# Edge layers of a graph network: the radial weights of two tiles as two products of 64 rows, one on each half of the array, in place of one product with a block-diagonal matrix

## The chip, the cores and the metric

The kernel runs on one core of a Trainium2 chip. Its time is the device time of one execution in microseconds, lower is better. Before the change three runs gave 8992.46 (the median), 9030.67 and 8966.20 us. Engines are named as the profile names them: PE is TensorE's matmul, PEld its weight load, DVE VectorE, ACT ScalarE, POOL GpSimd, SP SyncE.

## The reference, cut to what matters

Four message-passing layers over 50,000 nodes and 50,000 edges in float32. Layers 1 to 3 have a stage over the edges. Their part that the change touches is the small network that turns each edge's scalars into the weights of its message:

```
h = silu(edge_scalars @ (Wfc1 / sqrt(fan)))      # fan 16, 8 or 64 -> 64
w = h @ (Wfc2 / sqrt(64))                        # 64 -> 192 (layers 1, 2) or 224 (layer 3)
mid0 = w0 * e0 * sh0                             # parts of w times the gathered node row
...
sums = segment_sum(mid, edge_dst)                # then small matrices
```

Everything else (layer norms, node stages, the attention of layer 0) is the same before and after.

## The kernel before, in words

Edges come in 98 chunks of 512, a chunk being four tiles of 128 edges. Each stage of the program is one pass over the 98 chunks, with a software pipeline written out by hand: every engine has a list of steps with a delay in chunks, and the steps of one round are issued in the order of that list. The loop is unrolled four chunks deep. The edge stages of layers 1, 2 and 3 are `edge_layer` (L408 on), each followed by a short `join` and a node stage. The order of an edge round of chunk t is:

- SP: `load_edges(t)` (edge indices L426, then, once `message(t-2)` is done, the destination rows L324, attributes L433 and edge scalars L435), then `store_sums(t-4)` (L332), which waits for ACT's copy of the result.
- POOL: `gather(t)`, four indirect DMAs (L451), after the indices of t are in.
- PE: `hidden(t)` (L466, one product with a block-diagonal first matrix, after the edge scalars are in), `sums(t-2)` (L486, 12 products of 128 columns, 16 in layer 3), `weights(t)` (L474), `second(t-3)` (L498, L500, L503 in layer 3, L505).
- ACT: the silu (L516), the copies of the sums (L534), in layer 3 a copy in the gathered rows (L522), `weights(t)`: the copy of the radial weights out of PSUM (L526), and the copy of the result (L539).
- DVE: `message(t-1)` (L357 to L380, on to L388 in layer 3), then `prepare(t)`: the segment matrix (L337) after `sums(t-2)`, and the attributes (L555), which wait for the gathered rows of t.

The scalars of a chunk lie in pairs of tiles: rows 0 to 63 of `hid_p` (after the silu) hold the hidden values of tiles 0 and 2, rows 64 to 127 those of tiles 1 and 3, each in 128 columns for one tile; columns 0 to 127 are tiles 0 and 1, columns 128 to 255 tiles 2 and 3. `fc2_` is a matrix of 128 rows with Wfc2 twice on its diagonal (`diagonal(fc2, fc2)`), so one product of 128 rows and 2*w_cols columns (384, in layer 3 448) gives both tiles of a pair. `hid_p` is the stationary operand, `fc2_` the moving one. Each float32 product stands in the trace as two passes, each a weight load and a matmul; 1176 passes for 588 products.

Of the kernel before, what the change touches and what calls it, by code (L numbers as in the profile page):

```python
# [26 lines left out]
P = 128  # L27
# [96 lines left out]
def pipeline(eng, chunks, stages):  # L124


    most = max(d for _, d in stages)
    lead = most + (-most) % 4
    rounds = (chunks - lead) // 4

    def static(t):
        for stage, d in stages:
            if 0 <= t - d < chunks:
                stage(Step(t - d, t - d, (t - d) // 2, (t - d) // 4))

    for t in range(lead):
        static(t)
    with eng.Fori(0, rounds) as i:
        for k in range(4):
            for stage, d in stages:  # L140
                c = lead + k - d
                stage(Step(i * 4 + c, c, i * 2 + c // 2, i + c // 4))
    for t in range(lead + 4 * rounds, chunks + most):
        static(t)
# [7 lines left out]
def gnn_kernel(nc, inp, out):  # L152
# [5 lines left out]
    def sb(name, shape, dt=F32, own=None):  # L158

        return (own or ctx).enter_context(nc.sbuf_tensor(name, shape, dt))  # L160

    def two(name, shape, dt=F32, own=None):
        return [sb(f"{name}_{k}", shape, dt, own) for k in range(2)]
# [16 lines left out]
    with ctx:  # L180
# [13 lines left out]
        def W(name, rows=None, cols=None):  # L194
            r, c = SHAPES[name]
            r0, r1 = rows or (0, r)
            c0, c1 = cols or (0, c)
            return w_all[r0:r1, OFFSETS[name] + c0:OFFSETS[name] + c1]
# [12 lines left out]
        radial = two("radial", [P, TILES, 224])  # L211
# [7 lines left out]
        psum = ctx.enter_context(nc.psum_tensor("banks", [P, 8, 512], F32))  # L219

        def bank(k, rows=P, cols=512):
            return psum[0:rows, k, 0:cols]
# [12 lines left out]
        def tiled(k, cols):  # L235

            return psum[:, k:k + 2, :].rearrange("p b (t c) -> p (b t) c", t=2)[:, :, 0:cols]
# [77 lines left out]
        def precompute(eng, *values):  # L315


            for v in values:
                if type(v) is not int:
                    eng.compute_val(v)  # L320
# [87 lines left out]
        def edge_layer(layer):  # L408
            fan, radial_scale, w_cols, parts, v_at = LAYERS[layer]
# [4 lines left out]
            with ExitStack() as own, nc.Block() as block:  # L414
                erow = [sb(f"erow_{layer}_{k}", [P, TILES, EROW + 65], own=own) for k in range(4)]
                mid = two(f"mid_{layer}", [P, TILES, parts * P], own=own)
                mid_t, hid_p = two(f"mid_t_{layer}", [P, parts, CHUNK], own=own), sb(f"hid_p_{layer}", [P, 2 * P], own=own)
# [40 lines left out]
                @block.tensor  # L458
                def _(pe):
                    def hidden(s):  # L460

                        precompute(pe, edge_in[s.slot].after(s.half + 1), hid_sb.after(s.g))
                        pe.wait_ge(ready.sem, 1)
                        pe.wait_ge(edge_in[s.slot].sem, edge_in[s.slot].after(s.half + 1))
                        pe.wait_ge(hid_sb.sem, hid_sb.after(s.g))
                        pe.matmul(bank(1, P, 2 * P), W(f"fc1_{layer}"), scal_e[s.slot][:, :],  # L466
                                  start=True, stop=True).then_inc(hid_mm.sem, 1)

                    def weights(s):

                        pe.wait_ge(hid_sb.sem, hid_sb.after(s.g + 1))
                        pe.wait_ge(w_sb.sem, w_sb.after(s.g))
                        for k in range(2):
                            last = pe.matmul(psum[:, 2 + k, 0:2 * w_cols], hid_p[:, k * P:(k + 1) * P],  # L474
                                             W(f"fc2_{layer}"), start=True, stop=True)
                        last.then_inc(w_mm.sem, 1)

                    def sums(s):

                        pe.wait_ge(mid_step.sem, mid_step.after((s.g + 1) * steps))  # L480
                        pe.wait_ge(agg_sb.sem, agg_sb.after(parts * s.g))
                        for k in range(parts):
                            if k == 3:
                                pe.wait_ge(agg_sb.sem, agg_sb.after(parts * s.g + 1))
                            for t in range(TILES):
                                last = pe.matmul(psum[:, SEG[k], t * P:(t + 1) * P],  # L486
                                                 mid[s.slot][:, t, k * P:(k + 1) * P], seg[s.slot][:, t, :],
                                                 start=True, stop=True)
                            last.then_inc(agg_mm.sem, 1)

                    def second(s):

                        pe.wait_ge(agg_sb.sem, agg_sb.after(parts * (s.g + 1)))
                        pe.wait_ge(res_sb.sem, res_sb.after(s.g))
                        post = tiled(6, AGG)
                        for t in range(TILES):
                            cut = slice(t * P, (t + 1) * P)
                            pe.matmul(post[:, t, 0:v_at + 96], mid_t[s.slot][:, 0, cut], W(f"pa{layer}"),  # L498
                                      start=True, stop=False)
                            pe.matmul(post[:, t, v_at:v_at + 96], mid_t[s.slot][:, 1, cut], W(f"pb{layer}"),  # L500
                                      start=False, stop=False)
                            if crossed:
                                pe.matmul(post[:, t, v_at:v_at + 96], mid_t[s.slot][:, 3, cut], W("pd3"),  # L503
                                          start=False, stop=False)
                            last = pe.matmul(post[:, t, v_at + 32:v_at + 96], mid_t[s.slot][:, 2, cut], W(f"pc{layer}"),  # L505
                                             start=False, stop=True)
                        last.then_inc(post_mm.sem, 1)

                    pipeline(pe, chunks, [(hidden, 0), (sums, 2), (weights, 0), (second, 3)])

                @block.scalar
                def _(act):
                    def hidden(s):
                        act.wait_ge(hid_mm.sem, hid_mm.after(s.g + 1))
                        act.wait_ge(w_mm.sem, w_mm.after(s.g))
                        act.activation(hid_p[:, :], bank(1, P, 2 * P), ACT.Silu, scale=radial_scale) \  # L516
                            .then_inc(hid_sb.sem, 1)

                    def weights(s):
                        if crossed:  # L520
                            act.wait_ge(rows_in[s.slot].sem, rows_in[s.slot].after(s.half + 1))
                            act.activation(erow[s.quad][:, :, EROW:EROW + 64], erow[s.quad][:, :, 1 + C0:1 + C0 + 64],  # L522
                                           ACT.Copy).then_inc(wrap_sb.sem, 1)
                        act.wait_ge(w_mm.sem, w_mm.after(s.g + 1))
                        act.wait_ge(mid_step.sem, mid_step.after((s.g - 1) * steps))
                        act.activation(radial[s.slot][:, :, 0:w_cols].rearrange("p (b t) c -> p b t c", b=2),  # L526
                                       psum[:, 2:4, 0:2 * w_cols].rearrange("p b (t c) -> p b t c", t=2), ACT.Copy) \
                            .then_inc(w_sb.sem, 1)

                    def sums(s):  # L530
                        act.wait_ge(post_mm.sem, post_mm.after(s.g - 1))
                        for k in range(parts):
                            act.wait_ge(agg_mm.sem, agg_mm.after(parts * s.g + k + 1))
                            act.activation(mid_t[s.slot][:, k, :], bank(SEG[k]), ACT.Copy).then_inc(agg_sb.sem, 1)  # L534

                    def second(s):
                        act.wait_ge(post_mm.sem, post_mm.after(s.g + 1))
                        act.wait_ge(sums_out[s.slot].sem, sums_out[s.slot].after(s.half))
                        act.activation(res[s.slot][:], tiled(6, v_at + 96), ACT.Copy) \  # L539
                            .then_inc(res_sb.sem, 1)  # L540

                    pipeline(act, chunks, [(hidden, 0), (sums, 2), (weights, 0), (second, 3)])

                @block.vector
# [1708 lines left out]
```

## Time and profile before

| | |
|---|---|
| time, median of three runs | 8992.46 us (8966.20 to 9030.67) |
| span of the profiled execution, first to last instruction | 8623.9 us |
| PE busy | 6524.1 us, 76% |
| PEld busy | 5791.9 us, 67% |
| DVE busy | 6173.8 us, 72% |
| POOL busy | 5083.8 us, 59% |
| ACT busy | 4113.7 us, 48% |
| edge stages of layers 1, 2, 3, about | 3960 to 4770, 5390 to 6190, 6985 to 7950 us of the span |

No time of its own stands with the profiled execution beyond its span; 368.6 us of the median lie outside that span. A busy share is an average over stages with different limits. Matmuls overlap and their ends are modelled, so how long a pass holds the engine is read from the distance of its start to the next one's, not from its duration.

### The profile page before, as it was taken

Reading aid. Unit: us, or ns where it says so; the run is one execution under the profiler, and the core shown is the slowest. Engines: PE = TensorE matmul, PEld = TensorE weight load, DVE = VectorE, ACT = ScalarE, POOL = GpSimd, SP = SyncE. Lnnn points to the kernel's source line nnn. Section 1 sums busy time; section 2 is a strip of 40 time slices with the busy share of each in tenths; the row PEclk is TensorE's granted clock in tenths of the full one; section 3 lists DMA queues with packets and bytes.
Section 4 is the critical chain, followed back from the end, with each engine's and each line's share of the span. In section 5 each row is a group of like instructions: output and inputs, shape, how many; then the busy total and the mean of one; then the engine's idle time right before and its main releaser. Section 6 shows DMA issues by size and latency. Waiting matters only on the chain. (4 is left out here: it accounts for less than half of the span.)

```text
span 8623.9 us, 182979 instructions
## 1 busy us (share of the span) xinstructions
PE 6524.1 (76%) x42580; PEld 5791.9 (67%) x42580; DVE 6173.8 (72%) x20276; ACT 4113.7 (48%) x9706; POOL 5083.8 (59%) x4620
## 2 busy tenths in 40 slices
PE   3667878775456888888999666999755579998555
PEld 2555666664446888887888566888755569998454
DVE  4666888886556888885665777566588867775777
ACT  1334555552223444454444677444466654544444
POOL 4667888884334555554554787555466644443777
PEclk9887888885558999999999888999888889999666
DMA  6883333336883333333554676444455544443555
GB/s 129 173 179 81 88 88 88 88 90 128 161 164 96 104 101 105 101 105 102 126 125 118 190 211 203 118 122 124 115 169 165 168 125 120 120 119 105 157 160 154
DMA packets 910283, 1117.55 MB, mean 130 GB/s; under 512 B 458518, under 2 KB 546422, under 8 KB 910032
## 3 DMA queue, kind: packets, MB, share of 16 engines
q1 hardware_dynamic: 728032, 812.69, 34.1%
q0 software_dynamic: 182144, 303.64, 15.7%
q8 instruction: 42, 0.69, 0.0%
q14 instruction: 65, 0.53, 0.0%
HBM read 650.35 MB, written 465.65 MB: 129 GB/s over the span
## 5 line engine op out<-in xcount | busy, mean ns | idle before, releaser
L451 POOL DMA_INDIRECT erow<-e_rows,edge_idx x1176 | 1245.5, 1059 | 1232.0 <-issue 1136.5
L671 POOL DMA_INDIRECT agg<-seg_rows,edge_idx x1568 | 1550.7, 989 | 664.2 <-issue 473.0
L720 POOL TENSOR_TENSOR stats<-stats,power 128x8 f32<-128x8 f32 (+1 forms) x588 | 757.6, 1289 | 730.9 <-DVE stats L708 306.2
L400 PE MATMUL banks<-w_all,xt 128*128 128x128 f32 (+1 forms) x2352 | 538.3, 364 | 642.8 <-DVE y_more L945 146.1
L486 PEld LDWEIGHTS banks<-seg,mid 128*128 128x128 f32 x7840 | 931.9, 194 | 15.6
L486 PE MATMUL banks<-seg,mid 128*128 128x128 f32 x7840 | 932.9, 277 | 0.0
L400 PEld LDWEIGHTS banks<-w_all,xt 128*128 128x128 f32 x2352 | 422.3, 243 | 725.6 <-issue 713.0
L534 ACT ACTIVATE mid_t<-banks 128x512 f32<-128x512 f32 x980 | 585.2, 597 | 316.5 <-PE banks L486 314.2
L403 PE MATMUL banks<-w_all,xt 128*128 128x128 f32 x3528 | 642.0, 332 | 0.0
L403 PEld LDWEIGHTS banks<-w_all,xt 128*128 128x128 f32 x3528 | 603.8, 248 | 0.0
L498 PE MATMUL banks<-w_all,mid_t 128*128 128x161 f32 (+1 forms) x2352 | 583.5, 330 | 2.8 <-ACT res L539 2.8
L539 ACT ACTIVATE res<-banks 128x644 f32<-128x644 f32 (+1 forms) x294 | 218.1, 742 | 687.4 <-PE banks L505 672.5
L1207 POOL DMA_INDIRECT work<-src_table,edge_idx x392 | 460.3, 1174 | 108.1 <-issue 108.1
L608 POOL DMA_INDIRECT row_of_dram<-where_back x196 | 245.5, 1252 | 386.4 <-DMA where_back<-place_dram 339.6
L738 ACT ACTIVATE xo<-y,stats 128x64 f32<-128x64 f32 (+1 forms) x1200 | 428.9, 442 | 72.3 <-DVE stats L727 67.4
L1207 POOL DMA_INDIRECT y<-dst_table,edge_idx x392 | 386.6, 986 | 119.4 <-issue 119.1
L474 PE MATMUL banks<-w_all,hid_p 128*128 128x384 f32 (+1 forms) x1176 | 454.2, 508 | 3.1 <-ACT hid_p L516 3.1
L738 ACT ACTIVATE xo<-y_more,stats 128x64 f32<-128x64 f32 (+1 forms) x1152 | 411.5, 442 | 72.7 <-DVE stats L727 72.1
L498 PEld LDWEIGHTS banks<-w_all,mid_t 128*128 128x128 f32 x2352 | 378.7, 191 | 89.2 <-issue 38.4
L505 PE MATMUL banks<-w_all,mid_t 128*128 128x64 f32 x2352 | 423.4, 262 | 0.0
L500 PE MATMUL banks<-w_all,mid_t 128*128 128x96 f32 x2352 | 420.8, 260 | 0.0
L337 DVE TENSOR_TENSOR seg<-dst_row,edge_idx 128x512 f32<-128x512 int32 x294 | 202.8, 690 | 272.2 <-PE banks L486 233.5
(275 smaller groups left out, 18230.6 us busy)
## 6 DMA issues: line engine op xcount, KB each, us to landing
x_rows<-xo SPq DMA_DIRECT2D x294, 324.0 KB
xin<-x_rows SPq DMA_DIRECT2D x294, 324.0 KB
e_rows<-ets SPq DMA_DIRECT2D x294, 322.0 KB
dst_row<-in_dst_flat SPq DMA_DIRECT2D x294, 256.0 KB
xin<-in_x SPq DMA_DIRECT2D x196, 324.0 KB
seg_rows<-res SPq DMA_DIRECT2D x196, 322.0 KB, 2.6
seg_rows<-res SPq DMA_DIRECT2D x98, 384.0 KB, 2.4
seg_rows<-res SPq DMA_DIRECT2D x98, 338.0 KB, 9.4
```

What stands on the lines that cost most here:

```text
L400: pe.matmul(flat[:, to + k * cols:to + (k + 1) * cols], of[:, k * P:(k + 1) * P], W(w_s), start=True, stop=True)
L403: last = pe.matmul(flat[:, to + 2 * cols + k * P:to + 2 * cols + (k + 1) * P], of[:, (2 + k) * P:(3 + k) * P], W(w_v), start=True, stop=True)
L451: pool.indirect_dma_start(erow[s.quad][:, t, 0:EROW], None, table, bass.IndirectOffsetOnAxis(idx[s.slot][:, t:t + 1], 0),).then_inc(rows_i ...
L474: last = pe.matmul(psum[:, 2 + k, 0:2 * w_cols], hid_p[:, k * P:(k + 1) * P], W(f"fc2_{layer}"), start=True, stop=True)
L486: last = pe.matmul(psum[:, SEG[k], t * P:(t + 1) * P], mid[s.slot][:, t, k * P:(k + 1) * P], seg[s.slot][:, t, :], start=True, stop=True)
L498: pe.matmul(post[:, t, 0:v_at + 96], mid_t[s.slot][:, 0, cut], W(f"pa{layer}"), start=True, stop=False)
L505: last = pe.matmul(post[:, t, v_at + 32:v_at + 96], mid_t[s.slot][:, 2, cut], W(f"pc{layer}"), start=False, stop=True)
L534: act.activation(mid_t[s.slot][:, k, :], bank(SEG[k]), ACT.Copy).then_inc(agg_sb.sem, 1)
L671: pool.indirect_dma_start(agg[s.quad][:, t, 0:SUM_COLS[layer]], None, seg_rows[layer], bass.IndirectOffsetOnAxis(idx[s.slot][:, t:t + 1], ...
L720: pool.tensor_tensor(st[:, at + n:at + 2 * n], st[:, at:at + n], power[:, 0:n], ALU.pow) \
L738: last = act.activation(to, of if at == 0 else of.rearrange("p (i c) -> p i c", i=3), ACT.Identity, bias=st[:, 40 + t:41 + t], scale=st[:, ...
L1207: pool.indirect_dma_start(to[s.slot][:, t, :], None, table, bass.IndirectOffsetOnAxis(idx[s.slot][:, first + t:first + t + 1], 0),).then_i ...
```

## The change

In `weights` of PE, the two products of 128 rows and 2*w_cols columns become four of 64 rows and w_cols columns. The half h of the rows (0 to 63 or 64 to 127) is multiplied with the block of `fc2_` on the same rows; half h writes into bank 2 + h, at columns k*w_cols of it. Before, the pair k wrote into bank 2 + k. So the order of tiles within the two banks is another one, and ACT's copy (one instruction, as before) writes its halves into other tiles of `radial`. Semaphores and the order of steps are the same.

```
 for k in range(2):
-    last = pe.matmul(psum[:, 2 + k, 0:2 * w_cols], hid_p[:, k * P:(k + 1) * P],
-                     W(f"fc2_{layer}"), start=True, stop=True)
+    for h in range(2):
+        last = pe.matmul(psum[:, 2 + h, k * w_cols:(k + 1) * w_cols],
+                         hid_p[h * 64:(h + 1) * 64, k * P:(k + 1) * P],
+                         W(f"fc2_{layer}", (h * 64, h * 64 + 64), (h * w_cols, h * w_cols + w_cols)),
+                         start=True, stop=True)
 last.then_inc(w_mm.sem, 1)
...
-act.activation(radial[s.slot][:, :, 0:w_cols].rearrange("p (b t) c -> p b t c", b=2),
+act.activation(radial[s.slot][:, :, 0:w_cols].rearrange("p (t b) c -> p b t c", b=2),
                psum[:, 2:4, 0:2 * w_cols].rearrange("p b (t c) -> p b t c", t=2), ACT.Copy)
```

## Rows read from the trace of the kernel before

**Rows 1.** Stretches of the three edge stages: length, busy time (count), clock, DMA share, GB/s.
```profile
core 0: us, PE busy (x) PEld busy (x) DVE busy (x) ACT busy (x) POOL busy (x), PEclk, DMA share, GB/s
4000.00:4600.00 600.00, 574.42 (x4191) 524.54 (x4190) 372.49 (x930) 281.76 (x465) 322.33 (x310) 1.00 0.51 126
5500.00:6100.00 600.00, 573.56 (x4170) 523.33 (x4170) 372.34 (x930) 281.37 (x464) 327.61 (x311) 0.99 0.50 123
7100.00:7800.00 700.00, 700.00 (x5170) 641.78 (x5170) 510.64 (x1183) 346.38 (x591) 317.46 (x295) 1.00 0.42 119
```

**Rows 2.** Timeline of PE in layer 1 (start, us, engine, line; merged), one round.
```profile
4301.31 2.84 PE L486 MATMUL banks<-seg,mid 128*128 128x128 f32 x24
4303.98 1.46 PE L474 MATMUL banks<-w_all,hid_p 128*128 128x384 f32 x4
4305.28 0.44 PE L498 MATMUL banks<-w_all,mid_t 128*128 128x161 f32 x2
4305.56 0.36 PE L500 MATMUL banks<-w_all,mid_t 128*128 128x96 f32 x2
4305.75 0.36 PE L505 MATMUL banks<-w_all,mid_t 128*128 128x64 f32 x2
4305.94 0.49 PE L498 MATMUL banks<-w_all,mid_t 128*128 128x161 f32 x2
```

**Rows 3.** The same in layer 3; the last row is the next round.
```profile
7302.05 0.65 PE L466 MATMUL banks<-scal_e,w_all 128*128 128x256 f32 x2
...
7306.11 1.67 PE L474 MATMUL banks<-w_all,hid_p 128*128 128x448 f32 x4
...
7307.62 0.49 PE L498 MATMUL banks<-w_all,mid_t 128*128 128x192 f32 x2
...
7311.54 0.65 PE L466 MATMUL banks<-scal_e,w_all 128*128 128x256 f32 x2
```

**Rows 4.** Waits in layer 3, 7100 to 7800 us (total us, times, longest).
```profile
DVE tmp L357 <- ACT radial L526: 132.6, 74, 1.9
...
DVE seg L337 <- PE banks L486: 50.7, 74, 0.7
```

**Rows 5.** Waits in layer 1, 4000 to 4600 us.
```profile
DVE attr L555 <- DMA erow<-e_rows,edge_idx: 123.7, 61, 5.0
...
PE banks L466 <- issue: 25.4, 33, 2.5
```

**Rows 6.** Timeline of layer 1 that ends in a late round.
```profile
4316.91 0.65 PE L466 MATMUL banks<-scal_e,w_all 128*128 128x256 f32 x2
...
4324.20 0.65 PE L466 MATMUL banks<-scal_e,w_all 128*128 128x256 f32 x2
...
4325.34 0.36 SPq L332 DMA_DIRECT2D seg_rows<-res  x1
...
4326.31 0.34 SPq L426 DMA_DIRECT2D edge_idx<-in_edge_idx  x1
...
4331.39 1.17 POOL L451 DMA_INDIRECT erow<-e_rows,edge_idx  x1 [4.26 <-issue]
...
4335.37 1.36 POOL L451 DMA_INDIRECT erow<-e_rows,edge_idx  x1 [0.30 <-issue]
...
4339.44 0.18 DVE L555 TENSOR_TENSOR attr<-attr,erow 128x24 f32<-128x24 f32 x1 [3.52 <-DMA erow<-e_rows,edge_idx]
...
4343.51 0.28 DVE L380 TENSOR_TENSOR mid<-radial,tmp 128x128 f32<-128x128 f32 x1
...
4344.02 0.33 SPq L324 DMA_DIRECT2D dst_row<-in_dst_flat  x1
...
4345.11 0.36 SPq L435 DMA_DIRECT2D scal_e<-in_scal_e  x1
...
4347.96 0.67 PE L466 MATMUL banks<-scal_e,w_all 128*128 128x256 f32 x2 [0.80 <-issue]
```

**Rows 7.** Timeline of the setup: products of 2 rows alternate with products of 128 rows.
```profile
87.67 1.22 PE L1975 MATMUL banks<-w_all 2*128 2x256 f32 x2
...
88.82 0.50 PEld L1976 LDWEIGHTS banks<-w_all 128*128 128x128 f32 x2 [0.65 <-issue]
88.82 1.22 PE L1976 MATMUL banks<-w_all 128*128 128x256 f32 x2
89.97 0.50 PEld L1975 LDWEIGHTS banks<-w_all 2*128 2x128 f32 x2 [0.65 <-issue]
89.97 1.22 PE L1975 MATMUL banks<-w_all 2*128 2x256 f32 x2
```

**Rows 8.** Durations, ns min/median/max, of two lines with 256 columns.
```profile
L1976 PE MATMUL banks<-w_all x8: 634/714/796, 86.5 to 94.0; 128*128 128x256 f32 x8
...
L466 PE MATMUL banks<-scal_e,w_all x588: 378/435/767, 3960.6 to 7909.6; 128*128 128x256 f32 x196
```

**Rows 9.** The setup as a stretch, columns as in rows 1.
```profile
80.00:95.00 15.00, 9.46 (x18) 4.67 (x18) 6.34 (x28) 0.00 (x0) 0.00 (x0) 1.00 0.00 1
```

## The prediction

> **What bounds the kernel now.** I read the stretches of the three edge stages first, since only they run the changed line [rows 1]. The reader is to see that PE is busy for the whole 700 us of layer 3, at clock 1.00, while DVE has 511 and POOL 317; in layers 1 and 2 it is busy for 574 of 600. Next the timeline, for the length of a round. In layer 3 one round is 7302.05 to 7311.54, 9.49 us, and PE has no gap in it [rows 3]; DVE waits twice in each round, for the radial weights (132.6 us in 74 rounds, 1.8 each) and for PE's sums (0.7) [rows 4]. So layer 3 is PE's alone, and what PE's round gains or loses the stage gains or loses.
>
> Layers 1 and 2 are of another kind. 310 gathers in 600 us are 77.5 rounds of four, so a round is 7.74 us; a round without a wait is 7.29 (4316.91 to 4324.20) [rows 6]. PE waits before `hidden` in 33 of some 78 rounds, 25.4 us together, and DVE waits 123.7 us in 61 rounds for gathered rows [rows 5]. One late round shows the chain [rows 6]: PE starts a round at 4324.20, and with that the result of the round before can be copied; the store is issued at 4325.34, the indices at 4326.31, the gathers run from 4331.39 to 4336.73, their rows release DVE at 4339.44, the message ends at 4343.79, this lets SP issue the loads from 4344.02 to 4345.11, and `hidden` starts at 4347.96. That is 23.76 us for three rounds, 7.92 each, and no product of `weights` lies in it. I walked back so from the last round of either stage: one round where PE hadn't waited, three where the message had waited for gathered rows. There are 48 such chains as this one, and of 184 rounds about 40 are PE's. A saving of PE is worth a quarter of itself here (49 of 196 rounds), and less as the saving grows; a loss is worth more and more of itself, about half at 0.3 us.
>
> **The change part by part.**
>
> Streams. The four passes of `weights` take 4303.98 to 4305.28, 1.30 us, in layers 1 and 2, so 0.325 a pass of 384 columns [rows 2]; in layer 3 7306.11 to 7307.62, 1.51 us, 0.378 a pass [rows 3]. After, there are eight passes of half the columns, 0.163 and 0.189. If nothing overlaps their sum is as before, 1.30 and 1.51. The columns alone would allow half, 0.65 and 0.75, if the two halves always ran side by side.
>
> Loads. Each pass brings its weight load, so there are four loads more in a round. 24 passes of 128 columns take 4301.31 to 4303.98, 0.111 each, and passes of 96 and of 64 columns follow one another equally fast (4305.56, 4305.75, 4305.94: 0.095 each): below some 100 columns the load is what is left [rows 2]. I take 0.11 for a load of 128 columns. Then eight passes can't start closer than 0.11: seven such steps and the last stream are 0.77 + 0.16 = 0.93 us, in layer 3 0.77 + 0.19 = 0.96, beside 1.30 and 1.51. In the order of the program both passes of a half follow each other and can't overlap, only the second of one half with the first of the other; laid out so, it is 0.94 and 0.99. I take these if the halves overlap at all. Bounds: nothing overlaps (1.30, 1.51), or loads overlap too (0.65, 0.75).
>
> Going over to 64 rows and back. The hot rounds have no such product, the setup has: two passes of 2 rows, two of 128, in turns [rows 7]. They start 1.15 us apart (87.67, 88.82, 89.97), and each time the load starts together with its matmul, after a gap of 0.65, where in the rounds loads run ahead of matmuls. Two passes of 256 columns at 0.325 for 384 are 0.43 at the full clock. The granted clock in the setup reads 1.00 [rows 9], but its passes last 714 ns where those of 256 columns in the edge stages last 435 at the full clock and at most 767 [rows 8], so I read the setup as running at the half clock: 0.87 for the two passes, 0.28 for going over. At the full clock I halve it, 0.14, as the passes themselves about halve (767 to 435); 0.28 is the upper bound, and zero the lower one, if 64 rows need no going over. The round has two of them: 0.28 us, bounds 0 and 0.56.
>
> The Trainium skill says on this, in TensorEngine Tiling (Array Packing), Key Properties, that a change of tiling mode drains TensorE; the trace agrees by the gap of 0.65 us in front of each load. By that rule without a price the sum keeps its term and not its size.
>
> ACT's copy reads the same banks with the same shape and writes the same number of values, and SP, POOL and DVE issue what they did. They cost nothing new. The copy starts when the last product ends, earlier or later with it, and DVE's next wait, 1.8 us for the radial weights in layer 3, moves along. DVE is busy for 6.9 of 9.49 us in a round (510.64 in 73.8 rounds) and stays free of the bound for any change below 1 us.
>
> Sum, with overlap and 0.28: layers 1 and 2, 0.94 + 0.28 = 1.22 for 1.30, -0.08; layer 3, 0.99 + 0.28 = 1.27 for 1.51, -0.24. In layer 3 this counts for about 96 of 98 rounds: -23 us. In layers 1 and 2 it counts for 49 of 196: -4 us. Together -27 us, on a span of 8623.9 that would be 8597; with the 368.6 us outside it the median of 8992.5 becomes 8965.
>
> **The rivals.**
>
> A. *No side-by-side work (slower).* The two halves run one after the other, because both passes of a float32 product hold it or because the halves share the stream. Then 0.28 a round is lost outright, from the first round on: layer 3 96 x 0.28 = 27 us, layers 1 and 2 half of 196 x 0.28 = 27 us, 54 together, 9047. It decides as soon as the overlap gives less than 0.28 us a round. For it: all passes on one engine stream in order, and no row of this trace shows two side by side. Against it: the two halves use different rows and different banks. With the upper price, 0.56, PE's round in layers 1 and 2 becomes 7.86 and passes the 7.74 of today; three quarters of 196 x 0.56 are 82, layer 3 54: +136, 9128. With overlap but the upper price it is +0.20 and +0.04: 20 + 4, 9016.
>
> B. *Overlap and no going over.* -0.36 and -0.52 a round: layers 1 and 2 45 x 0.36 = 16, layer 3 96 x 0.52 = 50, together -66, 8926. Against it speaks the gap in the setup, though that is for 2 rows, not 64.
>
> C. *Pairs run as one.* Both halves' loads and streams side by side, 0.65 and 0.75, no going over: -0.65 x 40 and -0.76 x 96 give -26 and -73, -99, 8893. With going over paid it is -0.37 and -0.48: -17 and -46, 8929. In layer 3 the loads by SP and the gather chain would have to hold a round of 8.7 us; their chain in layers 1 and 2 takes 7.92 a round, and with the longer message (DVE has 6.9 us a round for 4.8 [rows 1], so 2.1 more in three rounds) some 8.6, so I leave the gain whole.
>
> The Trainium skill has this one as a rule: in TensorE: Matmul & The Clock Gate, Part 3, products on different row groups run concurrently and start about 4 ns apart. No row of this trace shows it. The same part says that a load overlaps a running matmul only on other row groups; here the trace differs, as 24 passes on all 128 rows follow one another at 0.111 us with their loads under the stream before.
>
> D. *Nothing lands.* Layers 1 and 2 hide everything and layer 3's terms cancel: 8992.
>
> **How the numbers follow.** My forecast, overlap limited by loads with going over paid: 0.38. Overlap with the upper price or terms that cancel (D): 0.16. A at the lower price 0.18, at the upper 0.06. B and C with going over paid, 0.15. C in full 0.07. The predicted time is 8965. Its own range is 8940 to 8990. The range for 8 in 10 takes in 8893 at one end, without the case's own scatter, and A at the lower price at the other, with some 15 us of scatter: 8890 to 9062. About 1%, 90 us, is what a measurement of this kernel can tell from no change (its three runs span 64 us). Faster by more than that is C and a part of the scatter of B: 0.11. Slower by more is A at the upper price and part of the lower one: 0.10. Within: 0.79.
>
> **What the profile after would show.** From the first pass of L474 to L498 in layer 3: 1.27 us if I am right, 1.79 in rival A, 0.99 in B, 0.75 in C. The round of layer 3 is then 9.25, or 9.77, 8.97, 8.73, the same in each of its rounds. A gap in front of the first load of 64 rows and of the first of 128 rows shows the going over. In layers 1 and 2 rounds without a wait start 7.2 apart, PE waits before `hidden` longer than 25.4 us in 600, and the mean round stays above 7.6. Wrong would be a round of layer 3 that isn't PE's any more, a granted clock in the edge stages below 0.97, or a `weights` longer than 1.8 us.

## The result: half a per cent faster, and where it is in the profile after

Over 20 runs each the changed kernel takes 8941.58 us (8898.14 to 8998.47) and the kernel before 8987.16 (8920.23 to 9077.81); the ratio is 0.9948, 95% interval 0.9929 to 0.9968, or 45 us less (29 to 64). In a later measurement, 12 runs against 29, it was 8886.46 to 8926.31, ratio 0.9964 (0.9940 to 0.9989); the ratio leaves out two slow runs of the 29.

The spans of the two profiles don't show this: 8623.9 us before, 8936.7 after. The profiled execution after took 8938.53 us, so only 1.8 us lie outside its span. My 368.6 us outside the span of before was a misreading: that execution was itself a short one, by some 360 us, and no other run of the kernel before, of these 20 and those 29, took less than 8833.08. Most of it lies in code before layer 1 that the change doesn't touch: layer 1 starts at 3961 us of the span before and at 4294 after (last section). The comparison therefore goes stage by stage.

First the stretches of the three edge stages after the change (length, busy time and count of PE, PEld, DVE, ACT and POOL, clock, DMA share, GB/s), as [rows 1] are for before.

```profile
4400.00:5000.00 600.00, 562.57 (x4541) 524.77 (x4538) 378.02 (x940) 268.47 (x471) 325.49 (x313) 1.00 0.51 127
5800.00:6400.00 600.00, 560.51 (x4515) 522.30 (x4513) 378.84 (x940) 265.79 (x468) 324.40 (x311) 1.00 0.50 124
7400.00:8100.00 700.00, 695.76 (x5589) 658.94 (x5588) 520.59 (x1206) 341.08 (x606) 324.90 (x301) 1.00 0.46 123
```

In layer 3 PE, busy for all of 700 us before, now has gaps. Then the timeline of PE in one round of layer 3, the answer to [rows 3].

```profile
7722.48 0.65 PE L466 MATMUL banks<-scal_e,w_all 128*128 128x256 f32 x2
7722.96 3.73 PE L489 MATMUL banks<-seg,mid 128*128 128x128 f32 x32
7726.63 1.03 PE L475 MATMUL banks<-w_all,hid_p 64*128 64x224 f32 x8
7727.59 0.59 PE L501 MATMUL banks<-w_all,mid_t 128*128 128x192 f32 x2
...
7731.61 0.65 PE L466 MATMUL banks<-scal_e,w_all 128*128 128x256 f32 x2
```

The round is 9.13 us for 9.49. Its three parts: from `hidden` to `weights` 4.15 for 4.06 (+0.09), from `weights` to `second` 0.96 for 1.51 (-0.55), from there to the next `hidden` 4.02 for 3.92 (+0.10). Eight passes of 224 columns at 0.189 would be 1.51 us in a row, and they take at most 0.96 with the way back to 128 rows in it: the halves run side by side. The starts of the single passes, which the merged line hides, show it directly: they come in pairs 0.007 us apart (7726.627 and 7726.634), and the pairs follow one another at 0.189 (7726.921, 7727.110, 7727.299). Layer 1 shows the same, as in [rows 2]:

```profile
4654.13 0.92 PE L475 MATMUL banks<-w_all,hid_p 64*128 64x192 f32 x8
4654.98 0.54 PE L501 MATMUL banks<-w_all,mid_t 128*128 128x161 f32 x2
4655.35 0.36 PE L503 MATMUL banks<-w_all,mid_t 128*128 128x96 f32 x2
```

0.85 for 1.30, and 0.37 for 0.28 to L503 after it. Rounds without a wait take 7.05 us for 7.29.

What becomes of it is in the waits: first layer 1, 4400 to 5000 us (total us, times, longest), the answer to [rows 5].

```profile
DVE attr L558 <- DMA erow<-e_rows,edge_idx: 61.5, 51, 3.9
...
PE banks L466 <- issue: 32.9, 41, 1.6
```

PE waits longer before `hidden`, 32.9 us for 25.4, and DVE half as long for gathered rows, 61.5 for 123.7. Neither can be put down to the change: the second profile of the kernel before (below) has 17.8 and 56.0 in 4500 to 5100 us. Then layer 3, 7400 to 8100 us, the answer to [rows 4]:

```profile
DVE tmp L357 <- ACT radial L529: 86.7, 70, 1.3
DVE seg L337 <- PE banks L489: 73.1, 73, 3.5
...
ACT res L542 <- remote: 26.8, 6, 4.9
```

The last line is not in the same view of the first profile, but the change didn't bring it. The second profile of the kernel before has it more often, in 7600 to 8200 us:

```profile
ACT res L539 <- remote: 135.4, 29, 5.1
```

ACT's copy of the result waits for PE's last product of `second` and for the store of two chunks before. I read "remote" as that store landing late, and planned the three experiments with four buffers by it. The semaphore updates in the traces say otherwise. In all 6 of these waits after, and in all 29 of before_again, the update that the copy starts on, 0.02 to 0.11 us ahead of it, is PE's, and the store's semaphore had its last one over 15 us earlier. (The trace doesn't keep every update, but the copy starts as far behind PE's as in rounds without such a wait: in after, signal at 7581.01 and copy at 7581.11.) PE's last product of `second` had by its record ended 1.55 to 2.16 us before that signal. So the late thing is PE's signal and not a transfer. In the first profile PE's signals come at most 0.02 us after the product, in layer 1 (4000 to 4600 us) as in layer 3 (7100 to 7800).

Each stage from the first to the last start of `hidden`, 97 rounds, read from the timelines, with the best round of each (the first four rounds, in which the pipeline fills, left out; rows of the table that belong to the experiments are used below):

| kernel | layer 1 | layer 2 | layer 3 | best rounds, layers 1 and 3 |
|---|---|---|---|---|
| before | 751.8 | 749.4 | 920.0 | 7.29, 9.49 |
| after | 744.4 | 744.2 | 900.0 | 7.05, 9.14 |
| before_again | 752.7 | 749.9 | 951.9 | 7.29, 9.49 |
| full_split | 762.8 | 775.5 | 962.0 | 7.31, 9.50 |
| one_half | 777.1 | 765.2 | 963.6 | 7.69, 9.89 |
| half_by_half | 760.2 | 768.1 | 922.1 | 7.05, 9.14 |
| after_again | 754.8 | 741.6 | 900.3 | 7.04, 9.14 |
| narrow | 752.6 | 743.5 | 907.4 | 7.04, 9.13 |
| after_store5 | 769.0 | 750.5 | 937.0 | 7.04, 9.14 |
| before_store5 | 742.3 | 717.6 | 922.5 | 7.29, 9.49 |
| only3 | 761.8 | 756.7 | 915.0 | 7.29, 9.14 |
| after_res4 | 767.8 | 754.4 | 915.5 | 7.05, 9.14 |
| after_deep | 802.6 | 774.5 | 944.1 | 7.04, 9.14 |
| before_deep | 725.1 | 775.1 | 927.5 | 7.29, 9.49 |

The best rounds of one kernel agree to 0.02 us between executions. The lengths of the stages differ by up to 3.5% between two executions of one kernel (layer 3 of before and before_again). Between the first two profiles the three stages are 7.4, 5.2 and 20.0 us shorter, 33 together, which lies in the interval of the runs.

### The profile page after: what moved, and what is told of

Its sections match the earlier page's. It is cut to its first block and busy times, and to the rows that moved or that the text cites. A ratio compares the mean times of both kernels' runs of the same rounds, so it can differ in the third digit from the quotient of the medians.

```text
span 8936.7 us, 185331 instructions
## 1 busy us (share of the span) xinstructions
PE 6648.0 (74%) x43756; PEld 5967.4 (67%) x43756; DVE 6182.5 (69%) x20276; ACT 4070.6 (46%) x9706; POOL 5067.3 (57%) x4620
## 5 line engine op out<-in xcount | busy, mean ns | idle before, releaser
L489 PEld LDWEIGHTS banks<-seg,mid 128*128 128x128 f32 x7840 | 937.0, 194 | 35.3 <-issue 14.7
L537 ACT ACTIVATE mid_t<-banks 128x512 f32<-128x512 f32 x980 | 543.4, 599 | 442.1 <-PE banks L489 403.5
L501 PE MATMUL banks<-w_all,mid_t 128*128 128x161 f32 (+1 forms) x2352 | 613.5, 343 | 2.8 <-ACT res L542 2.8
L1210 POOL DMA_INDIRECT y<-dst_table,edge_idx x392 | 443.2, 1131 | 119.5 <-issue 119.1
L1210 POOL DMA_INDIRECT work<-src_table,edge_idx x392 | 404.2, 1031 | 109.1 <-issue 109.1
L503 PE MATMUL banks<-w_all,mid_t 128*128 128x96 f32 x2352 | 421.1, 260 | 0.0
L1217 POOL TENSOR_TENSOR stats<-stats,power 128x12 f32<-128x12 f32 (+2 forms) x100 | 226.5, 2265 | 327.0 <-DVE stats L1404 302.3
L1291 PE MATMUL banks<-w_all,mid 128*128 128x128 f32 (+1 forms) x1176 | 180.7, 294 | 304.5 <-ACT mid_t L1357 241.5
```

The lines of the kernel that those rows point to most:

```text
L489: last = pe.matmul(psum[:, SEG[k], t * P:(t + 1) * P], mid[s.slot][:, t, k * P:(k + 1) * P], seg[s.slot][:, t, :], start=True, stop=True)
L1210: pool.indirect_dma_start(to[s.slot][:, t, :], None, table, bass.IndirectOffsetOnAxis(idx[s.slot][:, first + t:first + t + 1], 0),).then_i ...
```

## The experiments

Two theories on the step that decides. Mine at first: halves overlap, but loads and the order of the passes keep `weights` at 0.94 and 0.99 us. The rival: both halves run with loads and all side by side, 0.65 and 0.75, and going over costs more. The merged lines of the profile after can't tell which part of its 1.05 us (0.96, and 0.09 ahead of it) is stream and which is going over. So: the kernel before once more; more loads without 64 rows; 64 rows without anything to run beside; the order changed; the halves made unequal.

**before_again.** No edit.

> The kernel before, once more, to see what of the two profiles differs without any change. If the edge stages are as fixed as they look, the round of layer 3 is again 9.49 us in over 90 of its rounds, the mean rounds of layers 1 and 2 are 7.6 to 7.9, and the stage of layer 0 over the edges (650 to 2000 us in the first profile, 650 to 2300 in the one of the changed kernel) takes one of these two lengths. If the difference of the two layer-0 stages were caused by the change, this run would show the short one.

9083.16 us, beside 9161.21 for another run of the same kernel on that chip. Layers 1 and 2 are as in the first profile, and the stage of layer 0 took the long form without the change. But layer 3 was at its best round in 40 of 97 rounds, where the first profile had 94: I expected over 90. Layer 3 belonging to PE alone was true of one execution, not of the kernel. How a late round comes about can be read there: PE's signal of `second` comes 2.16 us after its product (7605.62), ACT's copy starts at 7607.89 after 5.14 us, the silu and ACT's copies of the sums come behind it, and PE stands for 0.73 us ahead of a product of `sums` (7609.51).

**full_split.** Eight passes on 128 rows.

```
-last = pe.matmul(psum[:, 2 + k, 0:2 * w_cols], hid_p[:, k * P:(k + 1) * P], W(f"fc2_{layer}"), ...)
+for h in range(2):
+    last = pe.matmul(psum[:, 2 + k, h * w_cols:(h + 1) * w_cols], hid_p[:, k * P:(k + 1) * P],
+                     W(f"fc2_{layer}", None, (h * w_cols, h * w_cols + w_cols)), ...)
```

> The kernel before with each product of weights split by its columns only: four products of 128 rows and w_cols columns, so eight passes and eight loads, no 64-row mode. Theory: loads hide under streams of 192 columns, so the round of layer 3 stays 9.49 us (weights 1.50), of layers 1 and 2 at best 7.29. Rival, if a load costs even beside a stream: 4 more loads at 0.11 give 9.93 and 7.73.

9209.49 us in one run. PE's timeline in layer 3:

```profile
8001.94 1.68 PE L475 MATMUL banks<-w_all,hid_p 128*128 128x224 f32 x8
8003.46 0.49 PE L500 MATMUL banks<-w_all,mid_t 128*128 128x192 f32 x2
```

1.52 us for eight passes, best rounds 7.31 and 9.50: four loads more cost 0.01 to 0.02 us. Loads on all 128 rows lie under the streams before them.

**one_half.** All four products on rows 0 to 63.

```
-hid_p[h * 64:(h + 1) * 64, k * P:(k + 1) * P], W(f"fc2_{layer}", (h * 64, h * 64 + 64), (h * w_cols, ...))
+hid_p[0:64, k * P:(k + 1) * P], W(f"fc2_{layer}", (0, 64), (0, w_cols))
```

> The changed kernel with all four products on rows 0 to 63 (the half of rows 64 to 127 is computed from the wrong half, so those values are not the reference's). Same passes, same going over to 64 rows and back, nothing that could run side by side. Theory (halves run side by side, worth half the stream; going over twice costs 0.40): layer 3 loses 0.75 against the changed kernel, round 9.89 us, weights from the last sum to the first product of second 1.90; layers 1 and 2 at best 7.70. Rival (the 64-row form is itself faster, or the going over cheaper, and nothing runs side by side): round 9.14 as in the changed kernel.

9184.85 us in one run. Layer 3:

```profile
8001.82 0.65 PE L466 MATMUL banks<-scal_e,w_all 128*128 128x256 f32 x2
8002.31 3.73 PE L489 MATMUL banks<-seg,mid 128*128 128x128 f32 x32
8005.97 1.78 PE L475 MATMUL banks<-w_all,hid_p 64*128 64x224 f32 x8
8007.68 0.59 PE L501 MATMUL banks<-w_all,mid_t 128*128 128x192 f32 x2
...
8011.71 0.65 PE L466 MATMUL banks<-scal_e,w_all 128*128 128x256 f32 x2
```

The round is 9.89, as the theory had it, and 1.71 between L475 and L501 for 0.96. The 0.75 between them is exactly half of the stream: the halves overlap fully. And 9.89 - 9.49 = 0.40 (in layer 1, 7.69 - 7.29 = 0.40) is the price of going over and back, with the same streams in both kernels. The starts of the single passes split it evenly. Going over, the first pass starts 0.205 us after the last of `sums` for the usual 0.112, and the second 0.294 after the first for 0.189; going back, the steps are 0.279 for 0.189 and 0.267 for 0.162. That is 0.20 us each way, and half of it is the second pass waiting: the load of the first starts together with its pass (8005.971 and 8005.973), it doesn't run ahead.

**half_by_half.** The loops swapped.

```
-for k in range(2):
-    for h in range(2):
+for h in range(2):
+    for k in range(2):
```

> The changed kernel with the two loops swapped: both products of rows 0 to 63 first, then both of rows 64 to 127, result the same. In program order only one pair of passes of different halves is adjacent. Theory A (the engine starts matmuls in program order, pairs need neighbours): of eight passes only one pair overlaps, weights takes 7 x 0.188 + 0.40 = 1.72, round of layer 3 9.7 us. Theory B (a half runs ahead of the other independently): 0.75 + 0.40, round 9.14 as in the changed kernel.

9126.94 us in one run, and theory B: 0.96 us again, best rounds 7.05 and 9.14.

```profile
8009.05 1.03 PE L475 MATMUL banks<-w_all,hid_p 64*128 64x224 f32 x8
8010.01 0.59 PE L501 MATMUL banks<-w_all,mid_t 128*128 128x192 f32 x2
```

Two whole products of one half precede the first of the other in the program, and still the first two passes start 0.013 us apart (8009.048 and 8009.061). My premise that only neighbouring passes can pair is wrong.

**narrow.** Only 64 columns in the products of rows 64 to 127.

```
+n = 64 if h else w_cols
-last = pe.matmul(psum[:, 2 + h, k * w_cols:(k + 1) * w_cols], ..., W(f"fc2_{layer}", ..., (h * w_cols, h * w_cols + w_cols)), ...)
+last = pe.matmul(psum[:, 2 + h, k * w_cols:k * w_cols + n], ..., W(f"fc2_{layer}", ..., (h * w_cols, h * w_cols + n)), ...)
```

> The changed kernel with only 64 of the w_cols columns in the products of rows 64 to 127 (the rest of those radial weights is not computed). Theory (the halves are two arrays with a queue each, the longer one sets the time): best rounds stay 7.05 and 9.14. Rival 1 (halves alternate in time and share the stream): 256 of 384 columns are left, weights is shorter by a third of 0.65, rounds 6.83 and 8.9. The durations of the 64-column passes also show which pass goes beside which.

8879.26 us in one run. Layer 3:

```profile
8009.89 1.02 PE L476 MATMUL banks<-w_all,hid_p 64*128 64x224 f32 x8
8010.84 0.59 PE L502 MATMUL banks<-w_all,mid_t 128*128 128x192 f32 x2
```

0.95 us, best rounds 7.04 and 9.13. The longer half sets the time; the halves don't share a stream.

Then the second question, where PE's saving goes: 0.24 x 196 + 0.35 x 98 = 81 us on PE, 45 in the runs. My theory was the gather chain, begun by indices that queue on SP behind a store that waits for PE.

**after_again.** No edit, measured beside the next two.

> The changed kernel beside the three others of this call, for their comparison. Theory: its best rounds are 7.05, 7.05 and 9.14 us again; how far the mean of a stage lies above its best round is set by the gathered rows, not by PE. It should be 30 to 60 us faster than the kernel before.

8886.46 us, 40 less than before (8926.31), or 32 by the ratio 0.9964. The best rounds are as expected. That gathered rows set the distance of the mean from them is not shown: layer 3 has 8 of the waits for PE's late signal in 500 us.

**after_store5** and **before_store5.** One edit, on the changed kernel and on the kernel before.

```
-pipeline(sp, chunks, [(load_edges, 0), (lambda s: store_sums(sp, s, s.g, layer, res), 4)])
+pipeline(sp, chunks, [(load_edges, 0), (lambda s: store_sums(sp, s, s.g, layer, res), 5)])
```

> The changed kernel with SP's store_sums one round later (delay 5 for 4), so that the load of the next indices doesn't queue behind a store that waits for PE's second. Theory (the gather chain hides PE's saving): the indices go out some 4 us earlier, the chain is off, and the mean rounds fall to within 0.2 us of the best ones, 7.1 to 7.25 and 9.15 to 9.3: about 0.5 x 196 + 0.1 to 0.5 x 98, 100 to 150 us faster than the changed kernel. Rival (the late rounds come from the DMA rings or from GpSimd's own pace, not from SP's order): mean rounds stay at 7.6 and above, no change.

> The kernel before with the same edit of SP's order. Theory: mean rounds 7.35 to 7.5 and 9.5 to 9.6, 70 to 110 us faster than before; and between this kernel and the changed one with the same edit the change is worth nearly its whole saving on PE, 0.24 x 196 + 0.35 x 98 = 81 us, where without the edit it is worth 30 to 60. Rival: the change's worth with the edit is the same 30 to 60.

On the kernel before: 8864.03 us, ratio 0.9950 (0.9919 to 0.9980), layers 1 and 2 at 742.3 and 717.6 us with mean rounds of 7.65 and 7.40. They are within 0.05 us of the best round in 67 and 87 rounds, in the two profiles without the edit in 39 to 43, so the chain was part of what held them. On the changed kernel: 8930.83, ratio to before 1.0028 (0.9998 to 1.0058), 44 us slower than without the edit. There too more rounds are at the best one (45 and 55 for 32 and 33), but nine rounds behind the fill take 11 to 15 us, where before_store5 has one. The wait in one of the nine, in layer 1:

```profile
4557.96 0.24 SPq L435 DMA_DIRECT2D scal_e<-in_scal_e  x1
...
4558.83 0.71 ACT L542 ACTIVATE res<-banks 128x644 f32<-128x644 f32 x1 [6.50 <-remote]
4559.44 0.38 ACT L519 ACTIVATE hid_p<-banks 128x256 f32<-128x256 f32 x1
4559.94 1.65 PE L475 MATMUL banks<-w_all,hid_p 64*128 64x192 f32 x8 [2.28 <-issue]
```

ACT stands for 6.50 us before the copy of a result, and the silu and PE's `weights` stand behind it. The store that the copy could wait for had its last update 11.3 us earlier; what comes at 4558.73 is PE's signal of `second`, whose last product had ended at 4553.90. In the 600 us from 4300 on PE's signals are up to 4.8 us late here and up to 4.6 in before_store5, so why the changed kernel has the long rounds and the other not is open. Both expectations failed: the edit gains 62 us on the kernel before, short of 70, and nothing on the changed one. So did the one that it brings out the change's full worth: with the edit the change costs 67 us (8864.03 to 8930.83), where without it it gains 40.

**after_res4**, **after_deep** and **before_deep.** Four result buffers for two, with four semaphores for the stores; in the two deep ones the store one round later as well.

```
-res = two(f"res_{layer}", [P, TILES, SUM_COLS[layer]], own=own)
+res = [sb(f"res_{layer}_{k}", [P, TILES, SUM_COLS[layer]], own=own) for k in range(4)]
...
-act.wait_ge(sums_out[s.slot].sem, sums_out[s.slot].after(s.half))
-act.activation(res[s.slot][:], tiled(6, v_at + 96), ACT.Copy) \
+act.wait_ge(sums_quad[s.quad].sem, sums_quad[s.quad].after(s.quarter))
+act.activation(res[s.quad][:], tiled(6, v_at + 96), ACT.Copy) \
```

> The changed kernel with four result buffers but the store in its old place. Theory (the indices still queue behind a store that waits for PE): layers 1 and 2 stay at mean rounds of 7.5 to 7.7; layer 3, where ACT waited for stores (8 waits, 34 us in 500), loses its late rounds and comes to 890 us. Rival (the buffers alone are enough): 7.1 to 7.25 in layers 1 and 2 too.

> The changed kernel with SP's store one round later and, besides, four result buffers for two, so that ACT's copy of a result waits for the store of four chunks ago and not of two. Theory (with the later store alone ACT waited for late stores, and with the old order the gather chain bound): both are off, the mean rounds come to within 0.2 us of the best, 7.05 to 7.25 and 9.15 to 9.3, the three stages 690 to 710 and 890 to 905 us, in all 100 us or more below the kernel before. Rival (late rounds come from DMA landing times, wherever they are waited for): stages stay near 745, 745, 900.

> The same two edits on the kernel before. Theory: rounds 7.29 to 7.4 and 9.49 to 9.6, stages 715, 712 and 925 us; the changed kernel with the same edits is then 60 to 81 us faster than this one, against 32 to 46 us without them. Rival: the distance stays at 32 to 46, so PE's saving is lost in something else than SP's order and the two result buffers.

9293.16, 9331.60 and 9220.75 us beside 9156.93 of the kernel before: ratios 1.0133 (1.0101 to 1.0165), 1.0153 (1.0107 to 1.0199) and 1.0071 (1.0042 to 1.0101). A good part of that lies in code ahead of layer 1 that none of them edits: `hidden` of layer 1 starts at 4530, 4519 and 4517 us, in only3, measured beside them, at 4403. Why, I can't say; the four further semaphores are the one thing I know of that reaches there, and no run has them alone. But the edge stages gained nothing either: after_res4 has 767.8, 754.4 and 915.5 us where only3 has 761.8, 756.7 and 915.0, so layer 3 didn't come to 890, and after_deep is the slowest of all in layer 1. In 400 us of it (4800 to 5200) stands:

```profile
ACT res L550 <- remote: 52.8, 7, 9.1
```

By the semaphore updates the stores are again not to blame: ahead of these 7 copies the store's last update was 24 us or more ago, and PE's signal came 3.6 to 7.0 us after its product. In layer 3 of after_res4 (7700 to 8400) there are 22 such waits, 103.8 us, with the store's last update 34 us ago. So four buffers couldn't help, since the two had held nothing up. My rival for after_deep, late rounds from transfers that land late wherever they are waited for, is not borne out by these waits either; what makes PE's signals late is open. The expectation that the change is worth 60 to 81 us with both edits failed by more than its size: after_deep is 111 us slower than before_deep (9331.60 to 9220.75), in the three stages 93.5. before_deep, with 725.1 us in layer 1 and 775.1 in layer 2 by the same code, shows how far one execution strays.

**only3.** The change in layer 3 alone.

```
+if crossed:
     for h in range(2): last = pe.matmul(... 64 rows ...)
+else:
+    last = pe.matmul(psum[:, 2 + k, 0:2 * w_cols], hid_p[:, k * P:(k + 1) * P], W(f"fc2_{layer}"), start=True, stop=True)
...
-"p (t b) c -> p b t c"
+"p (t b) c -> p b t c" if crossed else "p (b t) c -> p b t c"
```

> The change in layer 3 alone, layers 1 and 2 as before. Forecast from my steps: layer 3 is where PE sets the round, so most of the gain is there: stages 750, 750 and 900 us, some 20 to 35 us below the kernel before, against 32 to 46 of the whole change. Rival (the gain is spread as PE's saving is, 47 us in layers 1 and 2 and 34 in layer 3): less than half of the gain stays.

9107.24 us beside 9156.93, ratio 0.9931 (0.9892 to 0.9969). The rival, less than half of the gain, would be above 0.997, just outside. Layer 3 alone carries about half of it or more, and by this measurement perhaps all. Its profile had a slow layer 3, 915.0 us for the 900 expected, at its best round in 28 of 97. The interval is too wide to say what layers 1 and 2 add.

No kernel here is clearly faster than the changed one. before_store5, the kernel before with one number changed, has a median 22 us below it (8864.03 to 8886.46), and only3 is level with it.

## Why the prediction was right, step by step

8965 was forecast with 8890 to 9062, and a gain of 27 us; 8941.58 and 45 came. Two terms of the sum were mis-sized, and they partly cancelled; that the time came so near is in part luck.

- **Streams and loads.** I took 0.94 and 0.99 us for the eight passes, held by loads of 0.11 and by the order of the passes. Measured: 0.64 and 0.75 (7.69 - 7.05, 9.89 - 9.14), the bound I had set for the case that loads overlap too. My own terms didn't even give what I took: with starts no closer than 0.11, the passes of a half one after the other and a product's first pass behind the second of the one before, eight passes are 5 x 0.163 + 3 x 0.11 = 1.15 us, in layer 3 1.28, and with the loads running ahead from the first on still 0.99 and 1.04. The step that failed is "only the second of one half with the first of the other": half_by_half and narrow show that each half runs on by itself, and one_half that the overlap is worth the whole half of the stream. The rule that I had weighed as rival C, from the Trainium skill (TensorE: Matmul & The Clock Gate, Part 3), that products on different row groups run concurrently, was the right one; the trace now agrees, with eight passes in pairs 0.75 us shorter than the same passes on one half, and starts 0.007 us apart.
- **Going over.** I took 0.14 a time, halved from 0.28 in the setup. Measured: 0.20 a time, 0.40 a round. If the setup does run at half pace, as I read it, the cost falls from 0.28 to 0.20 and doesn't halve. The bounds 0 and 0.28 held it.
- **A round on PE.** -0.08 and -0.24 became -0.24 and -0.35. The case that came, pairs as one with going over paid, stands in my rival C with 8929 (it had -0.37 and -0.48 there, by the smaller price), within a chance of 0.15 shared with B. The likeliest case was not the true one; its time was near because of what follows.
- **What a saving is worth in layers 1 and 2.** A quarter, I said. 0.24 x 194 = 47 us on PE, and 12.6 between the first two profiles: 27%. Later profiles stray more than that (layer 1 of after_again is 754.8), so this is support and not proof. Only the direction is shown twice.
- **In layer 3.** All of it, I said: 0.35 x 97 = 34 us. The stage gained 20.0. It was at its best round in 94 of 97 rounds before and in 70 after, where PE's signals come late. before_again has 40 such rounds and the later signals without the change, so the missing 14 us can't be put down to the change; after_again, with 900.3, repeats the stage.
- **What was to be seen.** The granted clock stayed 1.00 in all three stretches, and the mean rounds of layers 1 and 2 above 7.6 (7.67 both). Rounds without a wait start 7.05 apart, not 7.2. `weights` to `second` in layer 3 is 0.96, near the 0.99 that I had given for rival B. That reading would have misled: 0.96 is not streams without a price, but 0.75 of streams and 0.21 of the way back, and another 0.19 stands ahead of L475 and behind L501. one_half told them apart.
- **The rivals.** A, no side-by-side work, is excluded: one_half is A as a kernel, at 9.89 a round. B fails by the 0.40.

## What to carry to other kernels

A float32 product whose moving matrix is block-diagonal in two halves pays its stream twice. Split on the array's halves it saves half the stream, and a visit to 64 rows cost 0.40 us here. By these two numbers, as an estimate, it breaks even at 0.40 / 0.5 = 0.80 us of stream a visit, so many products should share one. Ahead of such a change, count in how many rounds of a stage the engine is at its best round, in more than one profile. Measure an edit of the schedule on both kernels: one number gained 62 us on the one and lost 44 on the other. And where a view names no releaser ("remote"), look at which semaphore was updated last before you build on it; three of the experiments here rest on a wrong guess about it.

## What the runs showed of the hardware that I had not expected

- The two halves keep their own order only. In narrow, layer 1, the fourth pass of 64 columns starts at 4506.450 and the third of 192 at 4506.492, though the latter comes first in the program. The copy that waits for the semaphore on the last product started no less than 0.465 us after the start of the last pass of the longer half, as in the changed kernel (0.458), but for the fourth and the last round of layer 1, which are nearer in both (0.374 and 0.435, 0.367 and 0.446). So the signal did wait for both.
- Going over costs 0.20 us each way at a granted clock of 1.00 in the edge stages. The 0.28 of the setup is an estimate, as the prediction works it out.
- PE's signals can come late. In 7600 to 8200 us of before_again the signal of `second` comes a median 1.58 us after the end of its last product, 2.16 at most, and the signals behind it catch up: those of `second`, `hidden` and the first two groups of `sums` come at 7607.78, 7607.82, 7607.92 and 7608.01, though their products ended at 7605.62, 7606.11, 7607.00 and 7607.89. The signals of DVE and ACT, as far as the trace keeps them, come 0.01 us after the end in the same stretch. In the first profile PE's do too. The reason isn't shown.
- The stage of layer 0 goes at different paces in unchanged code: from the first to the last start of its first product (L1262) it takes 1278 us in the first profile and 1487 to 1636 in the thirteen others. Two stretches of it, first of before, then of before_again (columns as in the first fence):

```profile
1000.00:1200.00 200.00, 161.06 (x902) 125.84 (x902) 175.78 (x437) 105.86 (x302) 164.86 (x136) 0.85 0.33 89
```

```profile
1000.00:1200.00 200.00, 142.65 (x660) 115.67 (x660) 132.72 (x326) 80.20 (x223) 120.32 (x101) 0.72 0.25 68
```

PE does 902 passes in 200 us at a granted clock of 0.85, or 660 at 0.72. Layer 1 starts at 3961 us of the span in the first and at 4344 in the second, which is more than eight times the effect that was to be measured. Whether the clock is cause or consequence isn't shown.
